# Cross-attention scores as full-precision matmuls on eight 32x64 tiles, without the low parts of k and q

## The reference

```
q = (layernorm(x) @ Wq + bq)     # 16 heads of 16 channels
k = ctx @ Wk + bk;  v = ctx @ Wv + bv
a = clip(q @ k^T / 4, -10000, 10000);  p = softmax(a)   # 32 x 257 for each head and sequence
x = x + (p @ v) @ Wo + bo        # if any p is nan, p is 1/257 everywhere
```

## Time and profile before

| what | value |
|---|---|
| runs | 1110.69, 1109.12, 1103.54 us; median 1109.12 us |
| the profiled execution, span from its first to its last instruction | 1108.7 us (no time of its own is listed apart from the span; the span lies 0.4 us under the median) |
| TensorE busy | 995.9 us (90%), 10648 matmuls |
| VectorE, ScalarE, GpSimd busy | 783.6, 618.8, 651.1 us |
| granted TensorE clock, mean | 0.952 of 2.4 GHz |
| score matmuls (line 507) | 63.6 us busy, 768 of them |
| low parts of k (line 715) | 61.5 us of VectorE, 128 of them |
| query spreading (line 122) | 75.8 us of GpSimd, 128 of them |

### The profile page before, as it was taken

How to read it: one execution, slowest core, us unless ns; L and a number is a source line. 1 busy time by engine, 2 the same in 40 slices (tenths; PEclk the granted TensorE clock), 3 DMA queues, 4 the chain that set the end, 5 groups by cost and what they waited for, 6 DMA issues and landing times. The chain is left out here.

```text
span 1108.7 us, 29613 instructions
## 1 busy us (share of the span) xinstructions
PE 995.9 (90%) x10648; PEld 872.7 (79%) x10648; DVE 783.6 (71%) x2304; ACT 618.8 (56%) x1356; POOL 651.1 (59%) x806
## 2 busy tenths in 40 slices
PE   5899999999999997898999638999999518999998
PEld 3699999999999986786888527888878417988997
DVE  7477777777777778564566589776767487677884
ACT  2467666766666652533455486666656364444541
POOL 1387778777877881344666318777776213655443
PEclk9899999999999999898999859999999858999999
DMA  5222223222223213890000511333333348566501
GB/s 165 69 62 64 62 62 88 78 59 64 64 77 87 60 52 114 228 342 1 4 3 4 96 72 35 53 54 50 56 49 52 92 170 269 129 146 169 125 7 11
DMA packets 68636, 95.51 MB, mean 86 GB/s; under 512 B 12764, under 2 KB 48048, under 8 KB 68496
## 3 DMA queue, kind: packets, MB, share of 16 engines
q1 hardware_dynamic: 52464, 73.02, 21.1%
q0 software_dynamic: 16032, 20.62, 11.3%
HBM read 73.68 MB, written 22.18 MB: 86 GB/s over the span
## 5 line engine op out<-in xcount | busy, mean ns | idle before, releaser
L1926 POOL DMA_INDIRECT e_x<-rows,source x71 | 75.6, 1065 | 100.1 <-ACTq L1763 34.9
L737 DVE TENSOR_SCALAR xa_pT<-xa_ptp 128x512 f32<-128x512 f32 x128 | 88.1, 688 | 55.7 <-PE xa_ptp L517 55.7
L127 POOL TENSOR_TENSOR xa_cs<-xa_ctx,xa_cs 128x514 fp32r<-128x514 f32 x64 | 82.6, 1292 | 74.9 <-ACT xa_cs L676 74.8
L682 ACT ACTIVATE xa_pr<-xa_pr,xa_nm 128x257 f32<-128x257 f32 x256 | 108.7, 497 | 3.1 <-DVE xa_nm L733 3.1
L1937 POOL DMA_INDIRECT out_x<-e_y,target x32 | 54.1, 1690 | 74.3 <-DVE e_y L2714 63.0
L726 DVE TENSOR_SCALAR_CACHE_REDUCE xa_pr<-banks 128x257 f32<-128x257 f32 x256 | 93.6, 422 | 0.0
L2551 PE MATMUL e_hb<-e_xTs,e_w1s 128*128 128x512 f32 x384 | 90.9, 397 | 1.9 <-issue 1.9
L2605 ACT ACTIVATE e_h<-e_hb,rc_F_b 128x512 f32<-128x512 f32 x64 | 44.0, 688 | 87.1 <-PE e_hb L2551 87.1
L1931 POOL DMA_INDIRECT base<-e_y,place x39 | 69.7, 1788 | 36.5 <-DVE e_y L2209 20.7
L2567 PE MATMUL e_yb<-e_w2s,e_hTs 128*128 128x256 f32 x768 | 89.5, 278 | 0.0
L2567 PEld LDWEIGHTS e_yb<-e_w2s,e_hTs 128*128 128x128 f32 x768 | 88.2, 188 | 0.1
(11 more groups left out here) (360 smaller groups left out, 2894.3 us busy)
## 6 DMA issues: line engine op xcount, KB each, us to landing
e_w<-in_F_W SPq DMA_DIRECT2D x16, 1024.0 KB, 10.0
w<-in_W SPq DMA_DIRECT2D x24, 512.0 KB, 10.0
xa_ctx<-in_ctxT SPq DMA_DIRECT2D x32, 257.0 KB, 3.5
xa_ctx<-in_ctxT SPq DMA_DIRECT2D x64, 128.5 KB, 3.6
xa_vb<-vlx SPq DMA_DIRECT2D x64, 128.0 KB
rows<-xs_oT SPq DMA_DIRECT2D x4, 516.0 KB, 10.3
xs_oT<-in_x SPq DMA_DIRECT2D x4, 512.0 KB, 5.6
base<-xs_oT SPq DMA_DIRECT2D x4, 512.0 KB, 3.1
```

The lines of the kernel that those rows point to most:

```text
L127: pool.tensor_tensor(o["cs"][:, par, 1, :, 0:S], o["ctx"][:, slot, :, par, :], o["cs"][:, par, 0, :, 0:S], ALU.subtract).then_inc(o["cr_re ...
L682: act.activation(pr[:, par, g, :], pr[:, par, g, :], ACT.Exp, bias=nm[:, par, g:g + 1], scale=-1.0).then_inc(exp_ready, 1)
L737: dve.tensor_scalar(pT[:, par, 2 * h:2 * h + 2].rearrange("p g t c -> p (g t c)"), ptp[:], 1.0, None, ALU.min).then_inc(pT_ready, 1)
L1926: return pool.indirect_dma_start(out=out, out_offset=None, in_=rows, in_offset=bass.IndirectOffsetOnAxis(ap=index, axis=0))
```

## The change

The scores become matmuls of plain 32-bit floats. A sequence's k is stored once, by ScalarE, in full precision and with its running sum (`store_k`, which takes the place of `high_k` and `rest_k`); q likewise, so `rest` and `rest_k` on VectorE go. The queries are spread over tiles of 32 rows (2 heads) by 64 columns, in one operation per sequence of half the size of one of the two before. `scores` is eight matmuls of 257 columns, one for each strip of 32 rows and each half h; strip g writes bank g, half h writes 64 of its partitions. `s_ready` counts sequences instead of halves: all four clips wait for all eight tiles.

The order changes too. On VectorE `bounds` stands right behind the clips, then half 0 of the turned probabilities, then `store_output`. On ScalarE the exponentials stand ahead of `store_v`, half 0 of k and the context. On TensorE half 1 of `turn(b-1)` stands ahead of half 0 of `project_k(b+2)`. The layout of v, of the masks and of the last row's part follows the new places of the heads, with operations of the same sizes. The final test of `finite` is one operation with constants instead of one with two tensors.

The core of the diff (semaphores renamed or dropped along with it, masks and layouts are left out):

```diff
--- before
+++ after
...
          "ctx": m.sb("xa_ctx", [P, 2, 2, 2, S]), "cs": m.sb("xa_cs", [P, 2, 2, 2, SE], F32R),
-         "v": m.sb("xa_v", [P, 4, 2, G, 2, 33]), "qbd": m.sb("xa_qbd", [P, 2, 2, 2, P], F32R)}
+         "v": m.sb("xa_v", [P, 4, 2, 2, G, 33]), "qbd": m.sb("xa_qbd", [P, 2, 2, 2 * L])}
     for name in "eps_set rows_zeroed ones_ready pad_ready wh_ready wl_ready ch_pad_ready ch_ready cr_ready q_ready".split():
...
 def spread_queries(pool, o, w, qs, b, par):
-    msk = w["c_mask4s"][:].unsqueeze(1).unsqueeze(3).to_broadcast([P, 2, 4, L])
-    for a in range(2):
-        src = qs[:, a, :, bass.ds(b * L, L)].unsqueeze(2).to_broadcast([P, 2, 4, L])
-        dst = o["qbd"][:, par, a].rearrange("p h (e q) -> p h e q", q=L)
-        pool.tensor_tensor(dst, src, msk, ALU.mult).then_inc(o["q_ready"], 1)
+    msk = w["c_mask2s"][:].unsqueeze(1).unsqueeze(3).to_broadcast([P, 2, 2, L])
+    src = qs[:, :, bass.ds(b * L, L)].unsqueeze(2).to_broadcast([P, 2, 2, L])
+    dst = o["qbd"][:, par].rearrange("p h (e q) -> p h e q", q=L)
+    pool.tensor_tensor(dst, src, msk, ALU.mult).then_inc(o["q_ready"], 1)
...
                 rsqrt_refined(dve, rt[:, g], rs[:, g], tmp[:, g], step, 5 * h, ve[:, g])
-
-            def rest(c):
-                for h in range(2):
-                    dve.wait_ge(q_stored, 2 * c + h + 1)
-                    part = [qs[:, a, h, 512 * c:512 * c + 512] for a in range(2)]
-                    dve.scalar_tensor_tensor(out=part[1], in0=qp[:, c % 2, h, :], scalar=bq[:, h:h + 1], in1=part[0],
-                                             op0=ALU.add, op1=ALU.subtract,
-                                             accum_out=finite[:, 2 * B + 2 * c + h:2 * B + 2 * c + h + 1]
-                                             ).then_inc(rest_stored, 1)
...
             normalise(2)
-            rest(0)
             normalise(3)
             store_turned(2)
-            rest(1)
             store_turned(3)
-            rest(2)
-            rest(3)
...
                     act.wait_ge(qp_ready, 2 * c + h + 1)
-                    act.activation(qs[:, 0, h, 512 * c:512 * c + 512], qp[:, c % 2, h, :], ACT.Identity,
-                                   bias=bq[:, h:h + 1]).then_inc(q_stored, 1)
+                    act.activation(qs[:, h, 512 * c:512 * c + 512], qp[:, c % 2, h, :], ACT.Identity, bias=bq[:, h:h + 1],
+                                   accum_out=finite[:, 2 * B + 2 * c + h:2 * B + 2 * c + h + 1]).then_inc(q_stored, 1)
...
         vl = p.sb("xa_vl", [B, 4, D])
-        kT = p.sb("xa_kT", [P, 2, 2, 2, SE], F32R)
+        kT = p.sb("xa_kT", [P, 2, 2, S])
         vb = p.sb("xa_vb", [P, 4, D])
...
             def project_v(b, par):
-                pe.wait_ge(kl_ready, b * 2 + 1)
+                pe.wait_ge(k_ready, b * 2 + 1)
                 for t in range(2):
...
             def scores(b, par):
-                pe.wait_ge(q_ready, b * 2 + 2)
+                pe.wait_ge(q_ready, b + 1)
+                pe.wait_ge(k_ready, b * 2 + 2)
+                if not (static(b) and b == 0):
+                    pe.wait_ge(clip_ready, b * 4)
                 for h in range(2):
-                    pe.wait_ge(kl_ready, b * 2 + h + 1)
-                    if not (static(b) and b == 0):
-                        pe.wait_ge(clip_ready, b * 4 + (2 * h - 2))
-                    for n, (a, c) in enumerate(((0, 0), (0, 1), (1, 0))):
-                        for j in range(2):
-                            rows = slice(64 * j, 64 * j + 64)
-                            mm = pe.matmul(sc[:, 2 * h + j, 0:SE], qbd[rows, par, a, h, :], kT[rows, par, c, h, :],
-                                           start=(n == 0), stop=(n == 2))
-                    mm.then_inc(s_ready, 1)
+                    for g in range(G):
+                        rows = slice(32 * g, 32 * g + 32)
+                        mm = pe.matmul(sc[64 * h:64 * h + 64, g, 0:S], qbd[rows, par, h, :], kT[rows, par, h, :],
+                                       start=True, stop=True)
+                mm.then_inc(s_ready, 1)
             def turn(b, par, h):
...
                 if not static(b) or b < B - 1:
                     project_v(b + 1, 1 - par)
+                if not static(b) or b >= 1:
+                    turn(b - 1, 1 - par, 1)
                 if not static(b) or b < B - 2:
                     project_k(b + 2, par, 0)
-                if not static(b) or b >= 1:
-                    turn(b - 1, 1 - par, 1)
                 if not static(b) or b >= 2:
                     turn_output(b - 2, par)
...
             def queries(b, par):
                 if not (static(b) and b < 2):
-                    pool.wait_ge(s_ready, b * 2 - 2)
+                    pool.wait_ge(s_ready, b - 1)
                 spread_queries(pool, o, w, qs, b, par)
             def groups(a):
-                return a.rearrange("p (g c) -> p g c", g=G)
+                return a.rearrange("p (j g c) -> p j g c", j=2, g=G)
             def spread(a):
-                return a.unsqueeze(2).to_broadcast([P, G, 64])
+                return a.unsqueeze(1).unsqueeze(3).to_broadcast([P, 2, G, 32])
             def last_probability(b, par):
...
             act.wait_ge(w.loaded, w.total)
-            def high_k(b, par, h):
+            def store_k(b, par, h):
                 if not (static(b) and b < 2):
-                    act.wait_ge(s_ready, b * 2 - 2)
+                    act.wait_ge(s_ready, b - 1)
                 act.wait_ge(kp_ready, b * 2 + h + 1)
-                act.activation(kT[:, par, 0, h, :], kvp[:, (par + h) % 2, 0:SE], ACT.Identity,
-                               bias=bk[:, h:h + 1]).then_inc(kh_ready, 1)
+                act.activation(kT[:, par, h, :], kvp[:, (par + h) % 2, 0:S], ACT.Identity, bias=bk[:, h:h + 1],
+                               accum_out=finite[:, bass.ds(b * 2 + h, 1)]).then_inc(k_ready, 1)
             def high_context(b, par, slot):
...
                 if not static(b) or b < B - 1:
-                    high_k(b + 1, 1 - par, 1)
+                    store_k(b + 1, 1 - par, 1)
+                exponentials(b, par)
+                if not static(b) or b < B - 1:
                     store_v(b + 1, 1 - par, (2 * slot + par + 1) % 4)
                 if not static(b) or b < B - 2:
-                    high_k(b + 2, par, 0)
+                    store_k(b + 2, par, 0)
                 if not static(b) or b < B - 3:
                     high_context(b + 3, 1 - par, 1 - slot if par == 0 else slot)
-                exponentials(b, par)
             act.wait_ge(ones_ready, 4)
-            high_k(0, 0, 0)
-            high_k(0, 0, 1)
+            store_k(0, 0, 0)
+            store_k(0, 0, 1)
             store_v(0, 0, 0)
-            high_k(1, 1, 0)
+            store_k(1, 1, 0)
             high_context(2, 0, 1)
...
             dve.wait_ge(w.loaded, w.total)
-            def rest_k(b, par, h):
-                dve.wait_ge(kh_ready, b * 2 + h + 1)
-                dve.scalar_tensor_tensor(out=kT[:, par, 1, h, :], in0=kvp[:, (par + h) % 2, 0:SE], scalar=bk[:, h:h + 1],
-                                         in1=kT[:, par, 0, h, :], op0=ALU.add, op1=ALU.subtract,
-                                         accum_out=finite[:, bass.ds(b * 2 + h, 1)]).then_inc(kl_ready, 1)
-
-            def clip(b, par, h):
-                dve.wait_ge(s_ready, b * 2 + h + 1)
-                if h == 0:
-                    if not (static(b) and b < 2):
-                        dve.wait_ge(ptp_ready, b * 2 - 2)
-                        dve.wait_ge(plast_ready, b - 1)
-                for g in (2 * h, 2 * h + 1):
+            def clip(b, par):
+                dve.wait_ge(s_ready, b + 1)
+                if not (static(b) and b < 2):
+                    dve.wait_ge(ptp_ready, b * 2 - 2)
+                    dve.wait_ge(plast_ready, b - 1)
+                for g in range(G):
                     dve.tensor_scalar(pr[:, par, g, :], sc[:, g, 0:S], CLAMP, None, ALU.min, ALU.min,
...
                     invert(b - 2, par)
-                clip(b, par, 0)
-                clip(b, par, 1)
+                clip(b, par)
+                bounds(b, par)
+                if not static(b) or b >= 1:
+                    store_probabilities(b - 1, 1 - par, 0)
                 if not static(b) or b >= 3:
                     store_output(b - 3)
-                if not static(b) or b < B - 1:
-                    rest_k(b + 1, 1 - par, 1)
-                if not static(b) or b >= 1:
-                    store_probabilities(b - 1, 1 - par, 0)
-                bounds(b, par)
                 if not static(b) or b >= 1:
                     store_probabilities(b - 1, 1 - par, 1)
-                if not static(b) or b < B - 2:
-                    rest_k(b + 2, par, 0)
-
-            rest_k(0, 0, 0)
-            rest_k(0, 0, 1)
+
             dve.wait_ge(vlp_ready, 1)
...
                               ALU.mult).then_inc(vl_ready, 1)
-            rest_k(1, 1, 0)
```

(25 more changed lines are left out.)

3 lines of the change are left out of this document (removed).

## The result

The changed kernel takes 1103.84 us (median of 20 runs, 1098.4 to 1110.34) where the one before takes 1110.68 (median of 20 runs): the ratio taken over the runs, without one run of the kernel before that took 1946 us, is 0.9946, 95% interval 0.9931 to 0.9961. That is a real gain of about half a per cent, within the 1% called no change, and far from the 1086 us forecast. The profiled execution took 1107.39 us, its span 1105.1.

What follows compares the result with a forecast made beforehand. TensorE was taken to set the step: 5.83 to 5.48 us, 0.35 times 61 = 21.4, plus 0.6 in the query phase and 1 in the first steps, 23 off 1109.1: 1086 us, range 1075 to 1102.

Steps and rivals of the forecast that it cites:

- the release of turn half 1: VectorE's store of half 0 frees TensorE at 3.05 us of the step; the turn, ready at 2.94, waits 0.11.
- Two hand-overs: Between engines, scores to clips and store to turn half 1: 0.06 us each, from one row.
- the removal of the values' wait: TensorE's values: about 0.14 us of waiting for VectorE's store goes, leaving 1.04 of 1.18.
- `bounds` ahead of the store: VectorE: `bounds` takes 0.16 us, ends at 2.38; the store of half 0 runs 2.30 to 2.99.
- The scores: TensorE: eight f32 matmuls of 257 columns take 0.60 us in place of 0.92.
- Rival 1: Scores' weight loads not hidden: 0.2 us more, step 5.68, 9 us saved, with the ends 1098; chance 0.12.
- Rivals 2 and 3: Scores: strips take turns, 1.05, 1114 us, chance 0.06; a tile's passes run back to back, 2.2, 1185 us, 0.07.
- What costs nothing: Added or delayed work on ScalarE, GpSimd and SP stays covered; turns, layouts, masks, last test add nothing.
- The start: Query phase gains 0.6 us; first steps between 0 and 2, taken as 1.
- Tail: nothing: The kernel's end neither gains nor loses time.
- the wait's upper bound: Turn half 1 waits 0.23 us if `bounds` and store don't overlap and sums come a whole hand-over late.
- "faster": Whole kernel: chance 0.81 of being faster, from the forecast, the more-gained rival (1076 us) and half of Rival 1.

Runs made afterwards that it cites:

- e9: The changed kernel with each turn's two waits named in the other order, stored half first, exponentials second: 1098.43 us, 0.9883 of the kernel before.
- e1: The changed kernel with TensorE's old order put back, k half 0 ahead of turn half 1: 1097.47 us, 0.9872 of the kernel before.
- e6: The changed kernel with only `bounds` moved behind the store of half 0 on VectorE: 1094.1 us, 0.9848 of the kernel before.
- after: The changed kernel as the change made it, against the kernel before: 1103.84 us, ratio 0.9946.
- e2: The changed kernel with two of the five matmuls of k half 0 put ahead of turn half 1: 1097.99 us, 0.9875 of the kernel before.
- e3: The changed kernel with the context of sequences 4 and 5 asked for early in SyncE's order: 1095.85 us, 0.9887 of the kernel before.
- the filler: First half of the mean value's matmuls run twice in TensorE's last-step wait; alone on the changed kernel 1102.04 and, again, 1102.74 us.
- e15: As e13, with each turn's two waits in the other order: 1079.41 us, 0.9709 of the kernel before.
- e7: As e2, but `bounds` also writes an accumulator: 1087.78 us, 0.9793 of the kernel before.
- e13: The changed kernel with e2's split keys, accumulating `bounds`, e3's early context and the filler: 1082.39 us, 0.9756 of the kernel before.

## Why the prediction was wrong, point by point

**The step that failed is the release of turn half 1**, "it releases TensorE at 3.05". It was 3.21, and from it to the step's end 2.46 instead of 2.43: 5.67 instead of 5.48, 0.19 x 59 = 11 us. The mechanism was right, a wait behind which k half 0, the output's turn and the values stand; its size was not, and it decided. Two hand-overs were taken as 0.06 from one row, where a values' matmul follows a store with a single wait in front. From the scores' last result to the clips it was 0.11, and that result came at 0.69 instead of 0.67 (together 0.07); from the store to the turn 0.15 (0.09 more), the 0.09 gone when the two waits are swapped (e9). The sum stood close to an edge: with 0.25 of wait the new order costs 0.14 us a step against the old one (e1, 5.53), whose wait at the values is only 0.13. I took the removal of the values' wait as a gain without working out the old order with the new scores: 0.60 + 0.71 + 0.36 + 1.27 + 0.60 + 0.79 + 1.18 = 5.51 from the same rows. A comparison of 5.48 with 5.51 would have shown that the reordering could win 0.03 and hung on two hand-overs.

**`bounds` ahead of the store**: priced at 0.11 to the start of the store behind the clips, measured 0.12. Right, but that is not what it costs: without it in front the store overlaps the last clip (e6, 0.19 a step). Its length, 0.16 forecast, was 0.17 in 60 of after's 64 steps; in a shorter step it did not hold (e2).

**The scores**: 0.60 forecast, 0.62 measured, 16 per step on 32x64 tiles. Rival 1 fell: with weights loaded behind the first round the group would have been 0.8 by its estimate. The trace shows the loads too, line 488 alone in the columns of the earlier trace rows:

```profile
322.50:322.62 0.12, 0.12 (x8) 0.12 (x16) 1.00 0.00 0
322.74:322.86 0.12, 0.12 (x16) 0.00 (x0) 1.00 0.26 94
```

All sixteen weight loads have begun while only the first eight matmuls are in flight, which lie on all four strips, and all have ended before 322.74. So the measurement decides against the Trainium skill's rule as the prediction quoted it ("TensorE: Matmul & The Clock Gate", Part 3: Packing small matmuls). Rivals 2 and 3 fell with it (1.05 and 2.2).

**What costs nothing**: all covers held in after. The values wait for nothing; the exponentials start 2.51 into the step (2.44 forecast); the table of waits has no line for the output's turn, and ScalarE's waits for the context in 68 to 350 us are 0.6 us in all, 2 times, against 4.0.

**The start**: the query phase gained 0.8 (0.6 forecast): k's first projection starts at 34.56 instead of 35.36. The first steps gained nothing in the end: SP's order, which I had left out at the start, holds one load behind five transfers of other data, one write and four small loads (e3).

**Tail: nothing** was the other wrong term: +3.9 in both profiles of after, at half the clock, behind a wait that grew from 0.18 to 0.68 us. Without v's and k's projections in front of it, the last step has nothing to cover that loop. That the wait brought the clock down is not shown, since e1, e2 and e3 kept the clock behind the same wait.

On the profiled spans 3.6 us of the forecast 23 were gained. The missing 19.4 are 11.1 in steps 4 to 63 (20.7 forecast), 3.9 at the end, 1.4 up to step 4 (2.3 forecast, two steps of 0.35 among them, and 0.9 gained) and 3.0 in the untouched rest, which varies as much by itself. Without that rest it is 16.4; between the forecast and the medians lie 16.2. How much of the 3.9 is in the medians is not shown, since the filler moved them by only 1 to 2. The step of 5.67 is rival 1's 5.68, for another reason; the range ended at 1102, since the wait's upper bound, 0.23, was counted in the forecast's own range and not together with a loss at the ends; "faster" at 0.81 rested on one step time with nothing in it for hand-overs that no row of that kind showed.

## What to carry to other kernels

When a change shortens one engine's work, work out the old order with the new lengths first: here the old order with the new scores was 9 us faster than the change, and with part of the keys' work in front of the turn as cover, `bounds` with an accumulator, the waits swapped and both ends mended it is 24 us (e15). A hand-over in a loop over two engines is a term of its own, with its size from the same kind of instruction and the same number of waits. Look also at the first steps in the issuing queue, and at the last step, where the cover of the steady state is missing.

## What the hardware showed that I had not expected

- VectorE's 128x4 `bounds`, SBUF to SBUF, takes 0.17 us with GpSimd idle. In e2 it was over 0.2 us in 56 of 64 steps, 0.31 as a rule and 0.63 at most, and each time ended 0.02 to 0.03 us after a GpSimd instruction, mostly the sum; the form with an accumulator took 0.16 at the same overlap (e7). The Trainium skill says this ("SBUF — State Buffer", Who interferes with whom): a `tensor_scalar` can enter a mode that needs the port pair shared with GpSimd and then blocks until GpSimd's instruction ends, the form that writes its accumulator can't. The traces agree.
- The order in which two waits are named is worth 0.07 us a step where the awaited store comes last by 0.25 us (e9), and 0.04 where it barely does (e15 against e13). That an instruction with further conditions can have a separate instruction put in front of it for them is in the Trainium skill too ("Perfetto Trace Analysis", Identifying Dependency Chains); the price is from these runs.
- A row's named releaser was wrong 50 times of 50 (exponentials for the store) until the waits were swapped (e9).
